# Attention values divided by their sums between two 32x32 block transposes on VectorE, in place of TensorE transposes; rows of the output projection loaded in the matching order; body steps re-placed

## What is computed

```python
x = x + _layernorm(attn(_layernorm(x)))
x = x + _layernorm(ffn(_layernorm(x)))

def attn(x):                      # per batch, n = 512, H = 16 heads of 16, CH = 8 groups of 32 channels
    x = x + token_diffusion(_layernorm(x, ln1_w, ln1_b), Wqk_t, Wv_t, Wo_t, tau_t) * gamma1
    x = x + channel_diffusion(_layernorm(x, ln2_w, ln2_b), Wqk_c, Wv_c, Wo_c, tau_c) * gamma2

def token_diffusion(x, Wqk, Wv, Wo, tau):      # queries and keys are the same qk
    logits = (2 qk.qk' - |qk|^2 - |qk'|^2) / sqrt(16) * tau
    out = softmax(logits) @ v                  # each of 16 heads over 512 x 512
    return out @ Wo
```

## Time and profile before

| | us |
|---|---|
| median of 3 runs | 1119.0 (1118.0 to 1121.36) |
| profiled execution, its span | 1118.23, 1116.4 |
| PE busy | 1032.4 (92%) |
| ACT busy | 721.1 (65%) |
| DVE busy | 671.4 (60%) |
| POOL busy | 384.5 (34%) |
| granted TensorE clock, mean | 0.975 |

### The profile page before, as it was taken

One profiled execution on the slowest core, in us unless ns is written; L12 is line 12 of the kernel. 1 busy time (PEld: TensorE's weight loads), 2 busy tenths in 40 slices (PEclk: granted clock), 3 DMA queues, 4 the chain that ended last, 5 costly groups with the idle time before them and its releaser, 6 DMA issues. The chain is left out here.

```text
span 1116.4 us, 17406 instructions
## 1 busy us (share of the span) xinstructions
PE 1032.4 (92%) x5756; PEld 702.8 (63%) x5756; DVE 671.4 (60%) x1902; ACT 721.1 (65%) x1106; POOL 384.5 (34%) x353
## 2 busy tenths in 40 slices
PE   5899999999999999998899996999999999989966
PEld 3234545555455455544588875888888888878842
DVE  5225265454735645354785777677677776679927
ACT  2797767667776766666655662676677766768804
POOL 5121030513323141224426243444433443254315
PEclk9899999999999999999999987999999999989989
DMA  7673816427082542832433133334443344446456
GB/s 267 133 246 61 264 31 204 122 84 256 18 261 73 174 150 69 275 148 91 147 100 115 62 135 123 124 133 148 147 161 119 138 143 142 151 143 224 149 215 256
DMA packets 48960, 167.47 MB, mean 150 GB/s; under 512 B 10160, under 2 KB 16688, under 8 KB 42864
## 3 DMA queue, kind: packets, MB, share of 16 engines
q1 hardware_dynamic: 38170, 136.94, 36.9%
q0 software_dynamic: 10560, 29.14, 8.2%
q10 hardware_dynamic: 150, 0.41, 0.2%
HBM read 102.74 MB, written 63.70 MB: 149 GB/s over the span
## 5 line engine op out<-in xcount | busy, mean ns | idle before, releaser
L589 ACT ACTIVATE E<-PS,VV 128x1024 f32<-128x1024 f32 x256 | 271.6, 1119 | 73.7 <-PE PS L974 72.6
L1737 PE MATMUL PH<-XP,W1P 128*128 128x512 f32 (+1 forms) x1104 | 233.1, 369 | 4.9 <-DVE HP L1678 4.5
L1737 PEld LDWEIGHTS PH<-XP,W1P 128*128 128x128 f32 x1104 | 185.8, 192 | 44.5 <-DVE HP L1678 8.1
L974 PE MATMUL PS<-OPB,OPA 102*128 102x512 bf16 x512 | 137.9, 386 | 11.4 <-DMA OPB<-norm_parts 5.7
L1678 DVE TENSOR_TENSOR HP<-PH,HP 128x512 fp32r<-128x512 f32 x156 | 106.7, 686 | 64.8 <-ACT HP L1584 64.3
L957 PE MATMUL PO<-E,VA 128*32 128x512 f32 x1024 | 143.5, 610 | 0.0
L1579 ACT ACTIVATE PH<-PH,B 128x512 f32<-128x512 f32 (+1 forms) x184 | 107.5, 596 | 53.9 <-PE PH L1737 44.9
L1502 POOL DMA_INDIRECT choice_rows<-Y,DI x78 | 79.3, 1016 | 182.3 <-DVE Y L1635 160.8
L974 PEld LDWEIGHTS PS<-OPB,OPA 102*128 102x128 bf16 x512 | 37.7, 98 | 155.4 <-ACT E L589 68.7
L1570 ACT CAST W2P<-WG 128x512 fp32r<-128x512 f32 x92 | 56.9, 621 | 103.6 <-PE PB L1768 63.6
L462 POOL DMA_INDIRECT expert_rows<-PAY,SLOT x64 | 62.7, 979 | 157.5 <-issue 80.1
(11 more groups left out here) (254 smaller groups left out, 1611.2 us busy)
## 6 DMA issues: line engine op xcount, KB each, us to landing
expert_rows<-ZERO SPq DMA_DIRECT2D x8, 4160.0 KB, 12.8
WG<-experts SPq DMA_DIRECT2D x23, 1152.0 KB, 5.1
WG<-experts SPq DMA_DIRECT2D x23, 1028.0 KB, 5.2
OPB<-q_parts SPq DMA_DIRECT2D x192, 64.0 KB
YC<-choice_rows SPq DMA_DIRECT2D x8, 1024.0 KB, 13.0
q_parts<-QP SPq DMA_DIRECT2D x48, 128.0 KB
OPA<-q_parts SPq DMA_DIRECT2D x31, 192.0 KB
X<-x SPq DMA_DIRECT2D x8, 512.0 KB, 11.1
```

Of the source, the lines that this page charges most:

```text
L589: a.activation(E[:, s % 2, h, :, :], PS[:, u % 2, :, :], ACT.Exp, scale=vec("tau_t")[:, 4 * (s // 2) + h:4 * (s // 2) + h + 1]).then_inc(e ...
L974: ins = t.matmul(PS[:, u % 2, jc, :], OPA[0:KA, m, key:key + P], OPB[0:KA, m, hh * N:hh * N + N], start=True, stop=True)
L1737: last = m.matmul(PH[:, u % BANKS, at:at + w], W1P[:, a, k * HID + c * P:k * HID + c * P + P], XP[:, o, k, 0:w], start=(k == 0 and (a, o) ...
```

## The change

OT is no longer transposed on PE. DVE transposes it in 32x32 blocks: inside each group of 32 partitions and each 32 tokens, tokens come onto partitions and the 32 rows of one head onto columns, the sum's column among them. Two such transposes (L730 of the changed kernel), one reciprocal over both groups (L733), two multiplications (L736), which also pack the 16 value columns of two groups side by side, and one more block transpose (L739) give OTN with channels on partitions. One step of this kind, `untok0` or `untok1`, gives one half m of the channels. The intermediate tile TK is the memory of Z3T, TN that of ON. The channels of OTN stand in another order than before, therefore the rows of Wo are loaded in that order: eight DMAs of 16 rows each and one for the other three matrices, in place of one for all four.

The 24 PE transposes per batch, the four reciprocals and four multiplications from PSUM on DVE and ACT's two copies to OTN are gone, and with them the step `ontok`. PE's `proj` waits for a semaphore that DVE raises (`otn_ready`). In POST_AT, untok0 moves from position 2 to 1, untok1 from 3 to 2, and everything from proj on by one position forward; `residual` stays at 2. In TAIL_AT only `ontok` is gone. POST_USES goes from 18 to 12, and the numbers of the bank uses change with it.

```diff
-POST_AT = {2: ['residual', 'untok0'], 3: ['untok1'], 4: ['ontok'], 5: ['proj'], 6: ['z2'], 8: ['x2t'], 9: ['qkc'], 10: ['gram'],
...
+POST_AT = {1: ['untok0'], 2: ['residual', 'untok1'], 4: ['proj'], 5: ['z2'], 7: ['x2t'], 8: ['qkc'], 9: ['gram'],
...
-            sp.dma_start(WB[:, :, :, :], wview[:, 2:6]).then_inc(w_rest, 16)
+            sp.dma_start(WB[:, 1:4, :, :], wview[:, 3:6]).then_inc(w_rest, 16)
+            for h in range(H // KC):
+                q, g = h % 4, h // 4
+                at = 32 * q + DH * g
+                sp.dma_start(WB[at:at + DH, 0, :, :], wview[DH * h:DH * h + DH, 2]).then_inc(w_rest, 16)
...
-            def ontok(b, par):
-                for m in range(KC):
-                    a.copy(OTN[:, m, :], takep(b, 4 + m)).then_inc(post_free[m], 1)
-            do["ontok"] = ontok
-
...
                 if g == 0:
-                    at_least(act, post_full, POST_USES * (b - 1) + C)
+                    at_least(act, otn_ready, KC * b)
                 a.copy(OT[:, g, :], PO[:, :]).then_inc(po_read, 1)
...
-            def untok(half):
+            def untok(m):
                 def step(b, par):
 
-                    if half == 0:
+                    if m == 0:
                         post.at(b)
-                    for c in (2 * half, 2 * half + 1):
-                        ps = takep(b, c).rearrange("p (h e) -> p h e", e=32)
-                        post.did(v.reciprocal(REC[:, c, :], ps[:, :, DH]))
-                        post.wait()
-                        v.tensor_tensor(ON[:, c, :].rearrange("p (h e) -> p h e", e=DH), ps[:, :, 0:DH],
-                                        REC[:, c, :].unsqueeze(2).to_broadcast([P, H, DH]), ALU.mult).then_inc(post_free[c % 2], 1)
+                    dve.wait_ge(po_read, GROUPS * b + 2 * m + 2)
+                    for r in range(2):
+                        post.did(v.transpose(TK[:, r, :], OT[:, 2 * m + r, :]))
+                    post.wait()
+                    blocks = TK[:, :, :].rearrange("p r (j e) -> p r j e", e=32)
+                    post.did(v.reciprocal(REC[:, :, :], blocks[:, :, :, DH]))
+                    post.wait()
+                    for r in range(2):
+                        post.did(v.tensor_tensor(TN[:, m, :].rearrange("p (j r d) -> p r j d", r=2, d=DH)[:, r], blocks[:, r, :, 0:DH],
+                                                 REC[:, r, :].unsqueeze(2).to_broadcast([P, N // 32, DH]), ALU.mult))
+                    post.wait()
+                    v.transpose(OTN[:, m, :], TN[:, m, :]).then_inc(otn_ready, 1)
                 return step
...
-            def untok(half):
-                def step(b, par):
-                    pe.wait_ge(po_read, GROUPS * (b + 1))
-                    for c in (2 * half, 2 * half + 1):
-                        ps = givep(b, c)
-                        for g in range(GROUPS):
-                            i = t.transpose(ps[:, g * P:g * P + P], OT[:, g, c * P:c * P + P], ident)
-                        i.then_inc(post_full, 1)
-                return step
...
-            def ontok(b, par):
-                emptied(pe, b, 2)
-                emptied(pe, b, 3)
-                for m in range(KC):
-                    ps = givep(b, 4 + m)
-                    for c in range(C):
-                        i = t.transpose(ps[:, c * P:c * P + P], ON[:, c, m * P:m * P + P], ident)
-                    i.then_inc(post_full, 1)
...
-                emptied(pe, b, 4)
-                emptied(pe, b, 5)
-                rows_times(b, 6, OTN, lambda k: mat(wo, k))
+                pe.wait_ge(otn_ready, KC * (b + 1))
+                rows_times(b, 0, OTN, lambda k: mat(wo, k))
```

More of the change, by code:

```diff
@@ L39 @@
 KA = 102
-PRE_USES, POST_USES, LATE_USES = 7, 18, 4
+PRE_USES, POST_USES, LATE_USES = 7, 12, 4
 BEHIND = 3
@@ L77 @@
 TAIL_AT = {0: [('chan', B - 2)], 2: [('chan_add', B - 2), ('residual', B - 1)], 3: [('untok0', B - 1)], 4: [('untok1', B - 1)],
-           5: [('chan_stats', B - 2), ('ontok', B - 1)], 7: [('proj', B - 1)], 8: [('chan_norm', B - 2)], 9: [('z2', B - 1)],
+           5: [('chan_stats', B - 2)], 7: [('proj', B - 1)], 8: [('chan_norm', B - 2)], 9: [('z2', B - 1)],
            10: [('z3t0', B - 2)], 11: [('z3t1', B - 2)], 12: [('logits', B - 2)], 13: [('soft', B - 2)], 14: [('top', B - 2)],
@@ L559, in qkc @@
                 for i in range(2):
-                    a.copy(QC[:, 2 * i:2 * i + 2, :], takep(b, 10 + i).rearrange("p (c e) -> p c e", c=2)
+                    a.copy(QC[:, 2 * i:2 * i + 2, :], takep(b, 4 + i).rearrange("p (c e) -> p c e", c=2)
                            ).then_inc(post_free[i], 1)
@@ L564, in mixc @@
             def mixc(b, par):
-                a.copy(MB[:, :, :], takep(b, 14).rearrange("p (k e) -> p k e", k=2)).then_inc(post_free[0], 1)
+                a.copy(MB[:, :, :], takep(b, 8).rearrange("p (k e) -> p k e", k=2)).then_inc(post_free[0], 1)
             do["mix"] = mixc
             def weff(b, par):
-                a.copy(WE[:, :, :], takep(b, 15).rearrange("p (k e) -> p k e", k=2)).then_inc(post_free[1], 1)
+                a.copy(WE[:, :, :], takep(b, 9).rearrange("p (k e) -> p k e", k=2)).then_inc(post_free[1], 1)
             do["weff"] = weff
@@ L785, in dist @@
                 i.then_inc(post_free[1], 1)
-                emptied(dve, b, 13)
+                emptied(dve, b, 7)
                 post.wait()
@@ L1028, in tensor_program @@
             do["v0"], do["v1"] = vv(0), vv(1)
-            def untok(half):
-                def step(b, par):
-                    pe.wait_ge(po_read, GROUPS * (b + 1))
-                    for c in (2 * half, 2 * half + 1):
-                        ps = givep(b, c)
-                        for g in range(GROUPS):
-                            i = t.transpose(ps[:, g * P:g * P + P], OT[:, g, c * P:c * P + P], ident)
-                        i.then_inc(post_full, 1)
-                return step
-            do["untok0"], do["untok1"] = untok(0), untok(1)
-            def ontok(b, par):
-                emptied(pe, b, 2)
-                emptied(pe, b, 3)
-                for m in range(KC):
-                    ps = givep(b, 4 + m)
-                    for c in range(C):
-                        i = t.transpose(ps[:, c * P:c * P + P], ON[:, c, m * P:m * P + P], ident)
-                    i.then_inc(post_full, 1)
-            do["ontok"] = ontok
             def rows_times(b, j, lhs, rhs):
@@ L1081, in qkc @@
             def qkc(b, par):
-                emptied(pe, b, 8)
-                emptied(pe, b, 9)
-                rows_times(b, 10, X2T, lambda k: mat(wqkc, k))
+                emptied(pe, b, 2)
+                emptied(pe, b, 3)
+                rows_times(b, 4, X2T, lambda k: mat(wqkc, k))
             do["qkc"] = qkc
             def gram(b, par):
-                emptied(pe, b, 10)
-                emptied(pe, b, 11)
-                ps = givep(b, 12)
+                emptied(pe, b, 4)
+                emptied(pe, b, 5)
+                ps = givep(b, 6)
                 for k in range(2):
@@ L1099, in dist @@
                 pe.wait_ge(dg_ready, b + 1)
-                ps = givep(b, 13)
+                ps = givep(b, 7)
                 for k in range(2):
@@ L1108, in mixc @@
                 pe.wait_ge(at_ready, b + 1)
-                ps = givep(b, 14)
+                ps = givep(b, 8)
                 for k in range(2):
@@ L1115, in weff @@
             def weff(b, par):
-                emptied(pe, b, 14)
-                ps = givep(b, 15)
+                emptied(pe, b, 8)
+                ps = givep(b, 9)
                 for m in range(KC):
@@ L1125, in chan @@
             def chan(b, par):
-                emptied(pe, b, 15)
-                rows_times(b, 16, X2T, lambda k: WE[:, k, :])
+                emptied(pe, b, 9)
+                rows_times(b, 10, X2T, lambda k: WE[:, k, :])
             do["chan"] = chan
```

33 lines of the change are left out of this document (17 added, 16 removed).

## The result

The changed kernel took 1125.2 us (median of 13 runs, 1121.3 to 1130.72), the kernel before 1119.0 beside it (13 runs): ratio 1.0057, 95% interval 1.0033 to 1.0082. The profiled execution took 1125.15 us with a span of 1123.3, 6.9 us more than before.

The account below looks back on a forecast made before the run. PE was taken to set the first stage's pace, with DVE's queue near. Body 1 -3.3, bodies 2 to 6 0, clock +4.8, body 7 +2, slots +1.5: +5.0 us, predicted 1124 against 1119.0; range 1107 to 1134.

Parts of the forecast that it names:

- Body 1, -3.3 us: First body, without chan steps: untok1 ends ahead of PE's proj, so the full 3.3 us is gained.
- A step of 3.1 us, 0.69 us a transpose: One untok step on DVE: 3.1 us where reciprocals and multiplications took 1.25; a 512-column transpose 0.69 us.
- The hold-up of untok1's multiplications: Bodies 2 to 6: two-SBUF-input multiplications wait for POOL's residual, until 284.8 and 286.8; OTN ready at 287.9.
- PE waits 2.3 us at proj, steady bodies gain nothing: Bodies 2 to 6: PE reaches proj earlier, waits 2.3 us for OTN; net change 0.
- the waits at x2t and z3t0: Bodies 2 to 6, behind proj: PE waits about 1.7 us there for DVE's longer queue.
- Three falls of the clock, 4.8 us: Bodies 2 to 6: half-speed clock behind PE's waits, three falls at 1.6 us each, 4.8 us.
- Body 7, +2 us: Last body, no PRE work: PE waits some 6 us for OTN, delaying routing, scatter and gather; +2 us.
- Slots, +1.5 us: Numbered slots behind body 7: 3.7 us more DVE work, PE loses 2.7 us of transposes; -1 to +4, taken +1.5.
- The experts and the third stage: Behind the slots: as before, 0 us.
- Rival 1: First stage: PE keeps what it wins, no wait at proj, no clock fall; -13 us, 1106; chance 0.27.
- Rival 2: Bodies 2 to 6: the stall without clock falls; +0.2 us, 1119, no change; chance 0.20.
- Rival 3: DVE's transposes take 1.23 us instead of 0.69, +2.2 us per body; 1137; chance 0.11.

Follow-up runs that it names:

- experiment 1: Changed kernel with chan_add moved behind untok1 on DVE (position 2 instead of 1); ratio 1.0059 to the kernel before.
- experiment 4: Changed kernel with X1 in two buffers, POOL's residual at position 0, GS sharing MB's memory and zero rows in four DMAs; ratio 1.0188 to the kernel before.
- experiment 10: Changed kernel with the multiplications by the reciprocals replaced by copies, leaving out the division; ran once, 1114.0 us against 1120.1 for the kernel before.
- experiment 5: Changed kernel with the last body's own step table (untok1 at 4, proj at 6, z3t0 at 5) and TK in QR's memory; ratio 1.0046 to the kernel before.
- experiment 8: Changed kernel with untok0's two block transposes done twice, the same result written again; ratio 1.0182 to the kernel before.
- experiment 2: Changed kernel with the old positions: untok0 at 2, untok1 at 3, proj at 5, later steps one later; ratio 1.0074 to the kernel before.
- experiment 9: Changed kernel with the old positions in steady bodies and the last body's own table, first half not moved; ratio 0.9958 to the kernel before.
- experiment 3: Changed kernel with the first half's transposes, reciprocal and multiplications on DVE at position 14 of the batch's own body; ratio 0.9935 to the kernel before.
- experiment 6: Changed kernel with the first half's work at position 14 and the last body's own table; ratio 0.9857 to the kernel before.
- experiment 7: Changed kernel with first half at position 14, the last body's own table and old positions in steady bodies; ratio 0.9837, 1101.0 us against 1121.3 before.

## Why the prediction was right, and where it was not

**The forecast was +5.0 us and the profile shows +6.9**; the median moved by 6.2. The total is nearer than its terms: bodies 2 to 6 and what follows the slots came out 1.3 and 2.0 us below the forecast, body 7 and the slots 3.5 and 1.4 above, and that these partly cancel is luck.

- *Body 1, -3.3 us*: -2.9. Right.
- *A step of 3.1 us, 0.69 us a transpose*: untok0 takes 276.62 to 279.78, 3.16 us; a transpose alone 0.71, the pair 1.31. Right.
- *The hold-up of untok1's multiplications, one until 284.8 and the next until 286.8, OTN at 287.9*: 285.4, 287.5 and 288.2. Right, and shown by moving it: experiment 1 takes it away, experiment 4 moves it to untok0 and chan_add, and experiment 10 puts some 1.7 us a body on it. The ground given, that the old form reads PSUM and one SBUF tile and the new one two SBUF tiles, was too narrow: one SBUF tensor is enough to be held (experiments 4 and 10), as the scale instructions of rows 5 could have told.
- *PE waits 2.3 us at proj, steady bodies gain nothing*: 2.38 us, and body 4 has 66.33 us against 66.29. Right for these positions. Of the waits at x2t and z3t0, for which I gave 1.7 us, 1.13 were there (0.34 and 0.79). It holds only while steps stay where the change put them; at the old ones the bodies take 65.1 to 65.7 us. I had taken the order of the steps as given: chan_stats and split0 behind proj were 3.9 us in my chain (3.8 by its own terms). At the old positions they stand ahead of it again, and PE waits 1.06 us at proj and 1.27 at z3t0 in body 4; the body is 0.7 us shorter. No run moves them alone, so how much is theirs is not shown.
- *Three falls of the clock, 4.8 us*: three falls, in bodies 2, 3 and 5, each 1.4 to 1.7 us above body 4, 4.5 together. Right in the price; that there were three and not two is chance, since body 2 fell here and did not in experiment 5, with the same order there and the same wait (2.37 and 2.36 us). Body 6 was costed like the others and took 65.5 us, 1.0 less than before; it has no EARLY steps, and I did not look further into it.
- *Body 7, +2 us*: +5.5. This term was mis-sized. I had the wait (some 6 us; measured 5.29) but gave only 2 us for what it delays. The wait replaced 1.77 us and added 3.5 directly; then the clock was 0.91 over the body where it was 0.95, and PE's wait for the gather grew from 1.39 to 4.69 us. Experiment 5 wins 3.1 of it back with another order. How much of the growth is DVE's and how much the gather's own is open: experiment 8 has more DVE work and a body 7 of 74.1 us.
- *Slots, +1.5 us*: +2.9, inside the bounds given. The added wait is in front of the experts' product, which the prediction had not named: untok0 with its held pair stands ahead of HP on DVE, and PE waits 3.75 us for it. That wait is in experiments 1, 2, 5, 8 and 9 too (3.74 to 3.99), and in none of the three where the first half is done in body 7 (3, 6, 7), where PE waits some 2.0 us at proj in place of it. The experts and the third stage, for which I gave 0, took 2.0 less. What of these two is the clock stays open: no experiment held it constant.

Rival 1 (PE keeps its gain, -13 us, 1106) fell for the changed kernel, on the ground given for it: OTN would have had to be ready 2 us earlier. Experiments 6 and 7 provide that, with a last body of their own, and end below the ratio it gave (1106 to 1119 is 0.988). Rival 2 (the hold-up without the clock) is refuted by the three falls. Rival 3 (a transpose of 1.23 us) by the row of 0.71; experiment 8 shows that its price would have been higher than I gave: 1.3 us of DVE more per batch cost 14 us, where I had 13 us for 2.2 in each body.

## What to carry to other kernels

Work moved from a full engine to a half-empty one is a gain only if it does not land in the chain that the full engine waits for next: look for the place where the other engine is idle (here position 14, not 1), and for the earliest point at which its input is there. When one step changes its engine, every table that orders the steps is to be retuned, the special one of the last iteration too; there the full engine has less other work and meets the wait first. A wait of some 2 us on PE may cost more than itself: behind about half of such waits here the clock fell, which cost the changed kernel 1.4 to 1.7 us each time.

## What the runs showed of the hardware that was not expected

- A DVE block transpose (32x32, fp32) of 128x512 takes 0.71 us, and 0.6 to 0.65 from start to start in a row: about as long as the other 512-column fp32 instructions (0.67 to 0.69). It was not held up by a POOL instruction on SBUF tiles: 0.71 us beside L460 in experiment 4 (started 0.24 us behind it), and 0.71 beside L458 in experiment 10 (0.31 behind).
- Instructions with one SBUF tensor are held by POOL as well: a copy took 1.16 us, where the pair takes 0.49 elsewhere, and four scale instructions 2.96 us in place of 1.34. The copy behind it was not held by the next POOL instruction, while the second multiplication was. The copy started 0.01 us ahead of that POOL instruction and the multiplication 0.13 us behind it, but the scale instruction at 63.56 in the kernel before, 0.01 us ahead as well, was held: what decides, no run here tells.
- How long PE had waited does not alone decide whether the clock falls. In bodies 2 to 6 of all the kernels there was no fall where PE's longest wait was 1.65 us or less, and a fall in each one where it was 2.98 us or more (experiments 4 and 8). Between them both happened: 2.38 us in body 4 of the changed kernel without a fall and 2.09 in body 5 with one; 2.49 in body 3 of experiment 4 without, and 1.68 in body 5 of experiment 1 with one. In body 2 the same wait had a fall in the changed kernel (2.37 us) and none in experiment 5 (2.36).
